# Perceiver block on one core: attention with row-grouped scores, zero-padded values and a new order of the pipeline

## The reference

```
x = x + cross_attention(layernorm(x), ctx, ctx, mask)   # 16 heads of 8 features; scores / sqrt(8),
                                                        # masked ones to the lowest float, softmax, @ v, @ Wo + bo
x = x + recurrence(layernorm(x))                        # cumulative sums over 64 tokens, 32 hidden
x = x + experts(layernorm(x))                           # 4 layers, top-1 of 16 experts, 128 -> 512 -> 128
```

## Time and profile before

| | us |
|---|---|
| median of three runs (lowest, highest) | 622.74 (622.25, 626.61) |
| span of the profiled execution, from its first to its last instruction | 607.4 |
| TensorE busy, share of the span | 88% |
| VectorE, ScalarE, GpSimd busy | 60%, 50%, 35% |

### The profile page before, as it was taken

One profiled execution on the slowest core, in us unless ns is written; L12 is line 12 of the kernel. 1 busy time (PEld: TensorE's weight loads), 2 busy tenths in 40 slices (PEclk: granted clock), 3 DMA queues, 4 the chain that ended last, 5 costly groups with the idle time before them and its releaser, 6 DMA issues.

```text
span 607.4 us, 14280 instructions
## 1 busy us (share of the span) xinstructions
PE 536.6 (88%) x4254; PEld 437.6 (72%) x4254; DVE 364.3 (60%) x795; ACT 304.5 (50%) x732; POOL 214.7 (35%) x206
## 2 busy tenths in 40 slices
PE   2899999999996887799997699996899997699994
PEld 2678777877774563599963499973389994389992
DVE  3578787787877676645535745532944552954552
ACT  2567767676774831366621266631066650066550
POOL 3433242432420202541550640541362352363252
PEclk9799999999999987799999799996799999899999
DMA  5100000004930002110111110112010012010015
GB/s 134 29 11 18 9 9 17 9 17 137 332 94 2 0 1 70 32 36 7 41 60 42 26 38 10 36 39 71 5 45 24 23 37 83 1 49 24 18 42 151
DMA packets 30587, 27.73 MB, mean 46 GB/s; under 512 B 4608, under 2 KB 24384, under 8 KB 30528
## 3 DMA queue, kind: packets, MB, share of 16 engines
q1 hardware_dynamic: 26432, 18.59, 10.5%
q0 software_dynamic: 4096, 8.40, 4.8%
HBM read 20.68 MB, written 6.29 MB: 44 GB/s over the span
## 4 chain that ended last, share of the span: by engine, by line
PE 59%; DVE 18%; DMA 7%; issue 6%; ACT 6%; SPq 1%; POOL 1%; DVEq 0%; POOLq 0%; ACTq 0%
PE bank L748 19%; PE bank L761 18%; PE bank L564 5%; PE bank L592 3%; DVE nmax L858 3%; DMA cur<-token_rows 3%; ACT pp L420 2%; PE bank L573 2%; DVE rden L877 2%; DVE ohr L1047 2%; PE bank L543 2%; DMA token_rows<-ysort,token_i 2%; DMA qm<-token_rows,token_i 2%; PE bank L560 1%; PE bank L546 1%
## 5 line engine op out<-in xcount | busy, mean ns | idle before, releaser
L1096 DVE SCALAR_TENSOR_TENSOR hh<-th,bank 128x512 f32<-128x512 f32 x124 | 85.2, 687 | 118.8 <-ACT th L514 118.8
L761 PE MATMUL bank<-w,hh 128*128 x992 | 135.6, 280 | 3.0 <-DVE hh L1096 3.0
L748 PE MATMUL bank<-qm,w_piece 128*128 x992 | 134.8, 280 | 0.0
L761 PEld LDWEIGHTS bank<-w,hh 128*128 128x128 f32 x992 | 121.7, 193 | 4.6 <-issue 4.1
L748 PEld LDWEIGHTS bank<-qm,w_piece 128*128 128x128 f32 x992 | 122.5, 194 | 1.8 <-issue 1.3
L514 ACT ACTIVATE th<-bank 128x512 f32<-128x512 f32 x124 | 74.1, 597 | 84.8 <-PE bank L748 84.8
L505 ACT COPY w_piece<-w 128x512 f32 x124 | 75.8, 611 | 60.7 <-DVE piece_tile L1069 60.0
L323 POOL TENSOR_TENSOR qm<-qT,head_of 128x1024 f32<-128x1024 f32 x32 | 60.2, 1904 | 110.6 <-ACT qT L408 110.6
L361 POOL DMA_INDIRECT token_rows<-ysort,token_i x64 | 62.2, 971 | 101.1 <-DVE ysort L1106 94.8
L420 ACT ACTIVATE pp<-bank,nmax 128x128 f32<-128x128 f32 x256 | 73.5, 375 | 17.8 <-DVE nmax L858 17.8
L644 PE MATMUL bank<-trib,onesb 128*128 128x512 bf16 x308 | 82.2, 428 | 0.0
(11 more groups left out here) (186 smaller groups left out, 551.3 us busy)
## 6 DMA issues: line engine op xcount, KB each, us to landing
w<-in_L_ffn_W_dram SPq DMA_DIRECT2D x1, 4096.0 KB, 14.6
cur<-token_rows SPq DMA_DIRECT2D x16, 256.0 KB, 3.9
cx<-in_ctx_dram SPq DMA_DIRECT2D x16, 128.0 KB, 2.1
token_rows<-cur SPq DMA_DIRECT2D x1, 1024.0 KB, 5.1
qm<-token_rows,token_i POOLq DMA_INDIRECT x64
token_rows<-ysort,token_i POOLq DMA_INDIRECT x64, 2.2
out_dram<-xs SPq DMA_DIRECT2D x4, 256.0 KB, 2.8
xs<-in_x_dram SPq DMA_DIRECT2D x1, 768.0 KB, 5.7
```

The costliest lines, as they stand in the source:

```text
L748: last = mm(banks[2 + j % 2][:, c * P:(c + 1) * P], w1_piece[:, j % 2, c * P:(c + 1) * P], xT[:, ds(tile_of[j] * P, P)], start=True, stop= ...
L761: last = mm(banks[6 + j % 2][:, 0:D], hh[:, j % 2, c * P:(c + 1) * P], w2[:, ds(e * FF + c * P, P)], start=(c == 0), stop=(c == FC - 1))
L1096: v.scalar_tensor_tensor(hh[:, j % 2, :], th[:, j % 2, :], 1.0, banks[2 + j % 2][:, :], ALU.add, ALU.mult).then_inc(s["h_ready"], 1)
```

## The change

- Scores: the 128 features of q and k are four groups of 32 rows (four heads each). qm holds q four times a batch instead of sixteen, each copy keeping one head of every group (table `own_head`). Group r has bank r; its products are over 32 rows. Their mask products are over 64 rows, on the lower or the upper half of the array. They are issued in two halves, groups 0 and 1, then 2 and 3.
- Values: v is written into a zeroed tensor `vm` so that each head has a 32-column block with only its own 8 features. 64 products of 64 columns on four column groups then accumulate all heads and batches, with `head_ones` for the denominators, into one bank. `own_heads` and `diag` are gone; rows without any unmasked key are zeroed by `keep_any` in the residual's one instruction.
- Engines: `xln_tile` and the output bias go from VectorE to GpSimd; three of four copies of transposed probabilities go from ScalarE to VectorE.
- Banks and order: input transposes share bank 4 with the probabilities 0 and 3, v shares bank 5 with 1 and 2, and all orders are new. GpSimd's tiles are written out, and the last four tiles of the others.
- The mask is loaded twice, into both halves of the rows. `xin` and `xT` have memory of their own.

The diff, cut to its core:

```diff
@@ pairs_of_tiles
-            with eng.Fori(2, NT - 3, 2) as t:
+            with eng.Fori(2, NT - 5, 2) as t:
...
@@ constants (gpsimd)
-            g.memset(mask_bias[:], 0.0)
+            g.memset(head_ones[:], 0.0)
+            g.memset(vm[:], 0.0)
...
@@ gpsimd
+            def queries(t, u):
+                pool.wait_ge(s["qk_evac"], t + 1)
+                if not isinstance(t, int) or t >= 2:
+                    for r in range(4):
+                        pool.wait_ge(scored[r], t - 1)
                 for b in range(BT):
+                    last = g.tensor_tensor(
+                        qm[:, u, b, :, :], qT[:, u, b * S:(b + 1) * S].unsqueeze(1).broadcast_to([P, 4, S]),
+                        own_head[:].unsqueeze(2).broadcast_to([P, 4, S]), ALU.mult)
+                last.then_inc(s["qm_ready"], 1)
...
+            def pool_tile(t, u, first, last):
+                if not (isinstance(t, int) and t + 2 >= NT):
+                    queries(t + 2, u)
+                if not (isinstance(t, int) and t + 3 >= NT):
+                    if first:
+                        pool.wait_ge(s["rstd_ready"], 2)
+                    xln_tile(t + 3, 1 - u)
+                    add_out_bias(t + 3)
...
@@ scalar
             def tile(t, u, first, last):
+                if not (isinstance(t, int) and t + 1 >= NT) and not first:
+                    evac_qk(t + 1, 1 - u)
+                if not (isinstance(t, int) and t + 2 >= NT) and not first:
+                    evac_inputs(t + 2, u)
                 if not first:
+                    evac_pt3(t - 1)
+                for r in range(4):
+                    exp_scores(t, r, first)
...
@@ tensor
             def transposes_in(t, u):
                 pe.wait_ge(s["xln_ready"], t + 1)
                 pe.wait_ge(ctx_loaded[u], (t - u) * 8 + 16)
...
+            def scores(t, u, first, rs):
+                pe.wait_ge(s["qm_ready"], t + 1)
+                pe.wait_ge(s["qk_evac"], t + 1)
+                if not first:
+                    pe.wait_ge(s["exp_done"], 4 * (t - 1) + rs[-1] + 1)
+                for r in rs:
+                    half = slice((r % 2) * S, (r % 2 + 1) * S)
+                    mm(banks[r][:, :].rearrange("p (k t) -> p k t", k=4), pair_rows[half, :],
+                       mask_bias[half, :].unsqueeze(1).broadcast_to([S, 4, T]), start=True, stop=False)
                 for k in range(4):
+                    b, pair = k // 2, k % 2
+                    for r in rs:
+                        rows_of = slice(32 * r, 32 * r + 32)
+                        last = mm(banks[r][:, k * T:(k + 1) * T],
+                                  qm[rows_of, u, b, 2 * pair:2 * pair + 2, :].rearrange("p j s -> p (j s)"),
+                                  kT[rows_of, u, b * T:(b + 1) * T], start=False, stop=(k == 3))
+                        if k == 3:
+                            last.then_inc(scored[r], 1)
...
             def values(t, u):
+                pe.wait_ge(s["pt_evac_dve"], 3 * t + 3)
+                pe.wait_ge(s["pt_evac_act"], t + 1)
+                pe.wait_ge(s["v_evac"], t + 1)
+                if not isinstance(t, int) or t >= 1:
+                    pe.wait_ge(s["x_updated"], t)
                 for which in range(2):
+                    for b in range(BT):
+                        for j in range(4):
+                            at = (2 * b + j // 2) * P + (j % 2) * S
+                            for r in range(4):
+                                lhsT = vm[:, u, b * 4 + r, 32 * j:32 * j + 32] if which == 0 else head_ones[:, j, :]
+                                c = which * P + b * S
+                                last = mm(banks[6][32 * r:32 * r + 32, c:c + S], lhsT, ppT[:, r, at:at + S],
+                                          start=(which == 0 and b == 0 and j == 0),
+                                          stop=(which == 1 and b == 1 and j == 3))
                 last.then_inc(s["od_done"], 1)
...
             def tile(t, u, first, last):
+                if first:
+                    scores(t, u, first, (0, 1))
+                scores(t, u, first, (2, 3))
                 if not first:
+                    transpose_probs(t - 1, 3)
                 if not last:
+                    project_v(t + 1, 1 - u)
+                if not (isinstance(t, int) and t + 2 >= NT):
+                    project_qk(t + 2, u)
                 if not first:
+                    values(t - 1, 1 - u)
+                transpose_probs(t, 0)
                 if not first:
                     project_out(t - 1, 1 - u)
+                transpose_probs(t, 1)
+                if not (isinstance(t, int) and t + 3 >= NT):
+                    transposes_in(t + 3, 1 - u)
+                if not last:
+                    scores(t + 1, 1 - u, False, (0, 1))
+                transpose_probs(t, 2)
+            (ahead of tile 0: transposes_in 0 and 1, project_v(0), project_qk(0), project_qk(1), transposes_in(2))
...
@@ vector
             def values_evac(t, u):
+                dve.wait_ge(s["v_done"], t + 1)
                 if not isinstance(t, int) or t >= 2:
+                    dve.wait_ge(s["od_done"], t - 1)
+                v.tensor_tensor(vm[:, u, :, :].rearrange("p n (j x) -> p n j x", x=40)[:, :, :, 0:HD],
+                                banks[5][:, 0:BT * D].rearrange("p (n j d) -> p n j d", j=4, d=HD),
+                                bvr2[:].rearrange("p (n j d) -> p n j d", j=4, d=HD), ALU.add) \
+                    .then_inc(s["v_evac"], 1)
...
             def tile(t, u, first, last):
+                if not first:
+                    evac_pt(t - 1, 2)
                 scores_max(t, 0, first)
                 scores_max(t, 1, first)
+                if not last:
+                    values_evac(t + 1, 1 - u)
                 scores_max(t, 2, first)
+                scores_max(t, 3, first)
                 if not first:
                     attention_out(t - 1, 1 - u)
+                evac_pt(t, 0)
                 if not first:
                     residual(t - 1, 1 - u)
+                evac_pt(t, 1)
```

More of the change, by code:

```diff
@@ L165, in perceiver_block @@
         ctx_loaded = [sem(f"ctx_loaded{u}") for u in range(2)]
+        scored = [sem(f"scored{r}") for r in range(4)]
         gathered = [sem(f"gathered{u}") for u in range(4)]
@@ L187, in pairs_of_tiles @@
             body(1, 1, first=False, last=False)
-            with eng.Fori(2, NT - 3, 2) as t:
+            with eng.Fori(2, NT - 5, 2) as t:
                 body(t, 0, first=False, last=False)
                 body(t + 1, 1, first=False, last=False)
-            body(NT - 2, 0, first=False, last=False)
-            body(NT - 1, 1, first=False, last=True)
+            for t in range(NT - 4, NT):
+                body(t, t % 2, first=False, last=t == NT - 1)
         def layers(eng, body):
@@ L312, in _ @@
             g.memset(nf16[:, :, 0:1], 0.0)
[L313 to L317, removed]
+            for c in range(2):
+                g.tensor_tensor(pair_rows[:, c * S:(c + 1) * S], ident[:, 0:S], ident[:, S:P], ALU.add)
+            for j in range(4):
+                last = g.memset(head_ones[:, j, j * HD:(j + 1) * HD], 1.0)
@@ L331, in _ @@
+            pool.wait_ge(s["rstd_ready"], 1)
+            xln_tile(0, 0)
+            xln_tile(1, 1)
+            xln_tile(2, 0)
+            pool.wait_ge(s["w_loaded"], W_ATT)
+            for t in range(3):
+                add_out_bias(t)
+            pool.wait_ge(s["consts_dve"], 1)
+            queries(0, 0)
+            queries(1, 1)
+            for t in range(NT):
+                pool_tile(t, t % 2, t == 0, t == NT - 1)
             wait_normalised(pool, 0, 2)
@@ L408, in evac_qk @@
[L408 to L415, removed]
+                    act.wait_ge(s["qm_ready"], t - 1)
+                    for r in range(4):
+                        act.wait_ge(scored[r], t - 1)
@@ L416, in exp_scores @@
+                a.activation(qT[:, u, :], banks[7][:, 0:P], ACT.Identity, bias=bqc[:, 0:1],
+                             scale=float(HD) ** -0.5)
+                a.activation(kT[:, u, :], banks[7][:, P:3 * P], ACT.Identity, bias=bkc[:, 0:1],
+                             scale=1.0).then_inc(s["qk_evac"], 1)
+            def exp_scores(t, r, first):
+                n = 4 * t + r
                 act.wait_ge(s["nmax_ready"], n + 1)
-                if not (first and i < 2):
-                    act.wait_ge(s["pt_done"], n - 1)
+                if not first:
+                    act.wait_ge(s["pt_done"], n - 3)
@@ L433, in tile @@
+                if not (isinstance(t, int) and t + 2 >= NT) and not first:
+                    evac_inputs(t + 2, u)
                 if not first:
-                    evac_pt(t - 1, 2)
-                exp_scores(t, 0, first)
-                if not first:
-                    evac_pt(t - 1, 3)
-                if not last:
-                    evac_qk(t + 1, 1 - u)
-                exp_scores(t, 1, first)
-                evac_pt(t, 0)
```

(4 more changed lines are left out.)

295 lines of the change are left out of this document (115 added, 180 removed).

## The result

The changed kernel takes 739.29 us (median of 4 runs, 735.74 to 741.59), the kernel before 623.12 beside it: a ratio of 1.187 [1.181, 1.194], slower as forecast, but 49 us above the forecast of 690 and 9 above the upper end of its range of 650 to 730.

The account below looks back on a forecast made before the run. A ring of waits through four engines was taken to bound the changed kernel: 13.0 us a tile, 15.2 with 2.2 for the clock. The last projection comes 68 later, at 263; 622.7+68, say 690 us, range 650 to 730.

Parts of the forecast that it names:

- Direction and ring: Attention: slower by over 1% at 0.92; a circle of waits through TensorE, VectorE, ScalarE and GpSimd, 13.0 us a tile.
- The start: Start of attention: TensorE waits for tile 2's context load, so the second half of scores 0 starts at about 25.5.
- The clock: TensorE in attention: a low spell starts in each tile's gap, reaches 3 to 6 us into dense work, costs 2.2.
- change of shape: TensorE switching between full and 32-column or row-grouped products: 0.1 us each, 0.2 in each half of the scores.
- GpSimd's xln: GpSimd, behind the queries: making xln of one tile takes 0.35 us, the near end of its range.
- half-scores: TensorE: two masks at once, eight packed products and two shape changes make 1.29 us for a half of the scores.
- values: TensorE: 64 products of 64 columns on four column groups take 1.83 us a tile, as much as the 2.0 before.
- The sum: Attention: tiles 0 to 12 at 15.2 us, two at 12, then 16 to the last projection, at 263.
- Packing: TensorE's scores: two row groups run beside each other; a tile's scores take 2.58 us against 4.36.
- groups don't overlap: Rival for the scores: row groups run one after another, 1.1 us more a half, some 17 a tile, 718; chance 0.16.
- the rule of the Trainium skill: TensorE's values: about 62 ns per matmul instruction without hardware decoding, so 7.9 us instead of 1.8; the prediction set it aside.
- The faster rival: Attention: TensorE stays the bound, the ring closing under its own time, 9.4 us a tile, 605 in all; chance 0.05.

Follow-up runs that it names:

- filled: The changed kernel, order untouched, plus unread products: ten behind the transposes of probabilities 0, nine behind those of 1; 670.26 us, ratio 1.078.
- rows2: The kernel before, its 14 full products behind attention replaced by 14 sets of two 32-row products in two row groups; ran once, 607.96 us.
- both: The changed kernel with GpSimd's xln(t+3) ahead of queries(t+2), and VectorE's v bias behind maxima 2 and 3; 631.09 us, ratio 1.012.
- mid_fill: both, with tiles 2 and 3's context loads earlier, MLP weights behind tile 9's, five unread products before each of last four output projections; 608.89 us (0.979), again 599.49 (0.986).

## Why the prediction was right and wrong

- **Direction and ring: right.** The circle, its order through four engines and its length at full clock (13.0 forecast, 13.9 in filled) are what the traces show, and each edit at one arc shortened it. The start was right too: the second half of scores 0 was forecast at 25.5 and starts at 25.35.
- **The clock: this is the step that failed.** "The low spell begins in the gap and reaches 3 to 6 us into the dense part ... I take 2.2." It reaches 12 of the 13 us of that part and costs 4.9 us a tile (filled). The length was carried over from a spell of the kernel before that ended in full products; the new block is two fifths row-grouped (5.1 of 13.0 us, masks included), and in rows2 6.2 us of such work did not end a spell. That this is the reason in the block itself is inferred; that the spell lasts and what it costs is measured. The working had the change of shape in TensorE's time and not in its clock.
- **GpSimd's xln: mis-sized.** 0.35 was taken, the near end of a range up to 0.70; 0.79 is measured, above even the far end. GpSimd's add of the output bias, one operation on as many columns, takes 0.45 (L344), so the price of 128 columns, scaled down from 2,048 of them, was too low as well. With the queries at 0.59 each for 0.52 GpSimd's part of the ring is 0.6 us longer than forecast. On TensorE half-scores at 1.41 for 1.29, values at 1.97 for 1.83 and the transposes add 0.7, while VectorE's and ScalarE's parts are 0.4 shorter: together the 0.9.
- **The sum.** From the second half of scores 0 to that of scores 13 are 240.1 us, 18.5 a tile for the forecast 15.2: 42 us, of which the ring has 13 x 0.9 = 12 and the clock 30. From there to the last projection 48.7 for 40: 9, with the clock at 0.50 for 32 of the 48.7. Together the 51 us between 263 and 314.1, and the 49 between forecast and median.
- **Packing: right.** A half of the scores has 8 products, 16 instructions, on two row groups in 1.09 us, where 0.88 and a change of shape were forecast from the earlier trace rows; the two of a pair start 0.007 us apart. The rival "groups don't overlap" fell. So did the rule of the Trainium skill that the prediction names (TensorE: Matmul & The Clock Gate, the section on 56 against 53.3 ns), of about 62 ns an instruction without hardware decoding: 128 instructions of the values take 1.97 us, 15 ns each. The prediction's own reading against it was thin: fifteen instructions in 1.01 us are 67 ns each, and 58 only from start to start (236.79 to 237.66, where the next product begins). Whether this chip decodes in hardware, on which the rule depends, no run shows.
- **The faster rival** named the right place (the ring closing under TensorE's own time) with 9.4 us a tile. `both` opened the ring and has 10.1, as TensorE's own work is 8.9 and not 8.1. Even so it was no faster as a kernel until two loads were moved, which no part of the prediction had seen.

## What to carry to other kernels

When a pipeline is rewritten, walk once around each circle of waits over all engines before adding up any engine's work: here two lines, GpSimd's xln behind the queries and VectorE's v ahead of two maxima, cost 108 us. Products on half of the array saved time here, but in rows2 the clock stayed down under them; with the gap ahead closed (`both`, 60 to 140 us) or filled (filled, 0.98) it stayed up. And passes of many tiny products may ask for instructions faster than unrolled code gets them: look for issue waits there, and try moving large transfers away.

## What was unexpected of the hardware

- The granted clock stayed at 0.50 through 6.2 us of uninterrupted pairs of 32-row products and rose in 3.35 us with four of them side by side.
- TensorE waited, it seems for its own instructions: 2.99 us at the end of a loop beside a 290 GB/s transfer, none there without it; and 1.4 to 2.1 us further on in unrolled code in `both` and the kernels built on it, with no transfer.
- Nine to ten unread products at each of two places of a tile made the changed kernel 69 us faster.
- One execution of mid_fill had a granted clock of 0.65 nearly throughout and took 752 us, where the others took 606 to 613. Nothing here explains it.
